# First softmax stage of a graph network: edge attributes read in turned order, logits left in PSUM, row numbers kept on chip

## The chip, the cores and the metric

The kernel runs on one core of one Trainium2 chip. The metric is the device time of one execution in microseconds. "Before" is the kernel as it stood; its median over three runs is 21826.02 us (21825.98 to 21843.0). All times are of these runs, or of one profiled execution of the same kernel.

## What is computed

Four graph layers run one after the other over the same graph of 12500 nodes and 212500 edges, each followed by a residual sum and a layer norm. The change touches the second layer only:

```python
h   = node_h @ W_fc.T                      # 12500 x 64
eh  = edge_h @ W_fcr.T                     # 212500 x 64, edge_h = edge_attr_64
alpha = _segment_softmax(eh, dst, N)       # per node and per feature
agg = segment_sum(alpha * (h[src] + eh), dst, N)
h_new = where(deg > 0, agg + h @ loop_W, h)
return relu(h_new)
```

The edges come sorted by `dst`. All arithmetic is float32.

## The kernel before

The program is a sequence of phases with a barrier between them. Edges are padded to 128 x 1664: partition p holds 1664 consecutive edges (`NT = 1664`), and an edge phase walks over its columns in chunks. The phase of interest is `softmax_made("L1", ...)`, which takes `TL = 26` columns of every partition at a time, so 128 x 26 edges a chunk and `NC = 64` chunks. It forms the edges' logits by a matmul and makes a running softmax along each partition, so that each node's maximum and sums stand at its last edge. Each engine has its own loop over the chunks; two chunks (buffers 0 and 1) stand in one loop body. Semaphores set the order.

- **SP** (SyncE) issues all ordinary transfers of a chunk: `side` (the edge attributes, [128, 26, 64], L1724), `idx` (the 26 row numbers of the source nodes, L1732), the store of `M` (running maxima, L1736) and of `DN` (running sums, L1738). The order in the queue is: side and idx of chunk n, then M and DN of chunk n-2, then side and idx of chunk n+1, and so on. The idx load waits until the gathers of chunk n-2 have landed; the store of DN waits for ACT's copies.
- **POOL** (GpSimd) issues 26 indirect gathers a chunk in `gathers` (L926), one for each column: 128 rows of 256 bytes of the table `tab`, into `rows[b]`. It waits first for the idx transfer and until `rows[b]` was used (`valued`, chunk n-2). The same helper and the same line serve the other edge phases.
- **PE** (TensorE) transposes 13 blocks of 128 x 128 a chunk (two edge columns each; `turn`, L1764, into `pt`), in four groups of 4, 4, 4 and 1 blocks, and multiplies each turned block by a block-diagonal weight `bd["fcr"]` (`multiply`, L1773, into `lg`). A float32 multiply of one block is two pairs of instructions, weight load and matmul; a transpose is one pair. `pt` and `lg` have two buffers of one group each.
- **ACT** (ScalarE) copies each turned group from PSUM to `attrT` (`take`, L1793) and each product from PSUM to `eh[b]` (`make`, L1800), for the chunk ahead. Between them it does its part for the current chunk: `fades` (Relu and Exp, L1810 to L1815), `kill` (L1805), and `back` (two copies of the sums into `DN`, L1822).
- **DVE** (VectorE) runs a chain for each chunk: copy `eh` into `lx` in turned order (L1874), scan for the running maximum (L1878), `M` (L1882), `rows + logits` into `PV` (L1886, needs the gathered rows), difference (L1889, counts `dk`), then, after ACT's Exp, the weighting (L1894) and two scans (L1899), and the carried column (L1902, L1871).

The four groups of a chunk are interleaved on PE and ACT like this:

```python
def step(i, b):                               # PE
    pe.wait_ge(side_in[b], (i + 1) * 16)
    turn(i, b, 0)
    for g in range(NGR):
        if g + 1 < NGR:
            turn(i, b, g + 1)
        multiply(i, b, g)
```

A kernel of the same build is the last softmax phase, `softmax_flat("L3", ...)` (L1509 on): same chunk of 26 columns, same gathers (512-byte rows), same stores, but its logits are a difference of two loaded arrays and PE has no part in it.

If the edges did not come sorted, `sort_by_dst` would sort them and permute all edge arrays first. Whether it runs is decided on the device (L2379).

Of the kernel before, what the change touches and what calls it, by code (L numbers as in the profile page):

```python
# [5 lines left out]
I32 = mybir.dt.int32  # L6
# [13 lines left out]
T = 64  # L20
NT = -(-E // (P * 2 * T)) * 2 * T
# [11 lines left out]
def gnn_resnorm(nc, x_in, src_0, dst_0, attr3_0, attr64_0, w_0, w2_0, W, out):  # L33
# [36 lines left out]
    attr3_in, attr64_s = dram("attr3_d", [EP, 3]), dram("attr64_d", [EP, F])  # L70
    w_in, w2_in = dram("w_d", [EP]), dram("w2_d", [EP])
# [1035 lines left out]

    def sort_by_dst():
# [13 lines left out]
        permute("attr64", attr64_0, attr64_s)  # L1122

# [556 lines left out]
    TL = 26  # L1680

    @phase
    def softmax_made(name, idx_arr, table, last, lastmax):
# [5 lines left out]
        idx_in, rows_in, side_in = S("idx"), S("rows"), S("side")  # L1689
# [4 lines left out]
        turned, at_hand, product, made = q("turned"), q("at_hand"), q("product"), q("edge_logits")  # L1694
        GR = [(4 * g, min(4, TL // 2 - 4 * g)) for g in range(-(-TL // 8))]
        NGR = len(GR)
        with ExitStack() as c, nc.Block() as block:
            idx = [alloc(c, f"idx{b}", [P, TL], I32) for b in range(2)]
            rows = [alloc(c, f"rows{b}", [P, TL, F]) for b in range(2)]
            side = [alloc(c, f"side{b}", [P, TL, F]) for b in range(2)]  # L1700
            eh = [alloc(c, f"eh{b}", [P, TL, F]) for b in range(2)]
            aT_ = [alloc(c, f"attrT{z}", [P, 4, P]) for z in range(2)]
            pt, lg = ([ps(c, f"{n}{z}", [P, 4, P]) for z in range(2)] for n in ("pt", "lg"))
# [13 lines left out]
            def _(sp):  # L1717
                def load(i, b):
                    ch = i * 2 + b

                    def attr(array):
                        if not isinstance(i, int) or i:
                            sp.wait_ge(turned, (ch - 1) * NGR)
                        sp.dma_start(side[b][:, :, :], cols(array, ch, TL)).then_inc(side_in[b], 16)  # L1724
                    with sp.If(in_order > P - 1):
                        attr(attr64_0)
                    with sp.Else():
                        attr(attr64_s)
                    sp.end_ifs()
                    if not isinstance(i, int) or i:  # L1730
                        sp.wait_ge(rows_in[b], i * 16 * TL)
                    sp.dma_start(idx[b][:, :], cols(idx_arr, ch, TL)).then_inc(idx_in[b], 16)  # L1732

                def store(ch):
# [3 lines left out]
                    sp.dma_start(cols(sums2[0:EP, :], ch, TL), DN[:, :, :]).then_inc(sstored, 16)  # L1738
                load(0, 0)
# [11 lines left out]
            @block.gpsimd  # L1751
            def _(pool):
                gathers(pool, table, idx, rows, idx_in, rows_in,
                        lambda e, i, b: e.wait_ge(valued, i * 2 + b - 1), go, TL, NC)

            @block.tensor
            def _(pe):
                def turn(i, b, g):
                    h0, n = GR[g]
                    if not (isinstance(i, int) and i == 0 and b == 0 and g < 2):  # L1760
                        pe.wait_ge(at_hand, (i * 2 + b) * NGR + g - 1)
                    for h in range(n):
                        r = side[b][:, 2 * (h0 + h):2 * (h0 + h) + 2, :].rearrange("p a f -> p (a f)")
                        t = pe.transpose(pt[g % 2][:, h, :], r, ident[:, :])  # L1764
                    t.then_inc(turned, 1)

                def multiply(i, b, g):
                    n = (i * 2 + b) * NGR + g
                    pe.wait_ge(at_hand, n + 1)
                    if not (isinstance(i, int) and i == 0 and b == 0 and g < 2):  # L1770
                        pe.wait_ge(made, n - 1)
                    for h in range(GR[g][1]):
                        t = pe.matmul(lg[g % 2][:, h, :], aT_[g % 2][:, h, :], bd["fcr"][:, :], start=True, stop=True)  # L1773
                    t.then_inc(product, 1)
# [11 lines left out]
            def _(act):  # L1786
                def take(ch, g):
                    n = ch * NGR + g
                    w = GR[g][1]
                    act.wait_ge(turned, n + 1)  # L1790
                    if not (isinstance(ch, int) and n < 2):
                        act.wait_ge(product, n - 1)
                    act.activation(aT_[g % 2][:, 0:w, :], pt[g % 2][:, 0:w, :], ACT.Copy).then_inc(at_hand, 1)  # L1793

                def make(ch, b, g):
                    h0, w = GR[g]
                    act.wait_ge(product, ch * NGR + g + 1)
                    if g == 0 and not (isinstance(ch, int) and ch < 2):
                        act.wait_ge(formed, ch - 1)
# [738 lines left out]
```

## Time and profile before

| | |
|---|---|
| median of three runs | 21826.02 us |
| the profiled execution: its time | 21834.51 us |
| the profiled execution: its span | 21832.8 us |
| mean granted TensorE clock | 0.555 of full speed |
| POOL busy | 12097.6 us (55%) |
| DVE busy | 10276.4 us (47%) |
| PE busy / weight loads | 4275.1 us (20%) / 3247.4 us (15%) |
| ACT busy | 4673.7 us (21%) |
| traffic | 1517.57 MB, 70 GB/s in the mean |
| phase `softmax_made` | 12971.4 to 15917.8 us: 2946.4 us |

No engine is busy for most of the span. The busy share of an engine is a mean over some thirty phases which have different limits, so it says little about one of them; the phase of the change has to be read by itself. "Before" in a row means idle time of that engine just ahead of the instruction, and the arrow names what ended it. Releasers are inferred, and where a semaphore number was used for something else in an earlier phase, the name can be of that phase. Ends of matmuls are modelled.

### The profile page before, as it was taken

The page shows a single profiled execution, that of the slowest core. Times are in us where ns is not written, and L with a number is a line of the kernel's source. Part 1 is how long each engine was busy: PE and PEld are TensorE (multiplying, and loading weights), DVE is VectorE, ACT ScalarE, POOL GpSimd, SP SyncE. Part 2 cuts the span into 40 slices and gives each one's busy share as a digit, 9 for nine tenths or more (in the row PEclk, how much of TensorE's full clock was granted, in tenths as well). Part 3 has the DMA queues.
Part 4 walks back from the last instruction along what each step waited for, and adds up shares of the span by engine and source line. Part 5 has one row for each costly group of instructions (what it writes and reads, how often), then busy time and mean ns, then how long its engine had stood idle before and what let it go on. Part 6 is the DMA issues. An engine that isn't in the chain of part 4 may idle for free. (4 is left out here: it accounts for less than half of the span.)

```text
span 21832.8 us, 104239 instructions
## 1 busy us (share of the span) xinstructions
PE 4275.1 (20%) x22758; PEld 3247.4 (15%) x22758; DVE 10276.4 (47%) x18332; ACT 4673.7 (21%) x4961; POOL 12097.6 (55%) x12292
## 2 busy tenths in 40 slices
PE   1222224444434211111111111111111111100000
PEld 1111113333333210000000011111110000000000
DVE  4444445444444443333222235555555555567776
ACT  0100111111111002222233324333311111124442
POOL 4444443344343337776766655555555555467776
PEclk7555556766667655555555555555555555555555
DMA  2111111111111331111111113222222222234443
GB/s 63 37 37 36 35 41 50 46 39 47 39 48 43 121 141 53 53 52 52 48 53 54 52 56 94 94 94 94 91 62 65 64 64 64 57 108 141 141 141 111
DMA packets 583064, 1517.57 MB, mean 70 GB/s; under 512 B 276152, under 2 KB 276685, under 8 KB 539138
## 3 DMA queue, kind: packets, MB, share of 16 engines
q1 hardware_dynamic: 188414, 1028.89, 12.7%
q0 software_dynamic: 392160, 467.91, 9.9%
q10 hardware_dynamic: 2068, 16.12, 0.2%
q8 instruction: 146, 2.39, 0.0%
q14 instruction: 276, 2.26, 0.0%
HBM read 714.46 MB, written 803.57 MB: 70 GB/s over the span
## 5 line engine op out<-in xcount | busy, mean ns | idle before, releaser
L926 POOL DMA_INDIRECT rows<-tab,idx x6656 | 6650.0, 999 | 3734.1 <-issue 2170.6
L572 POOL DMA_INDIRECT moved_rows<-recs,sidx x1664 | 1619.0, 973 | 2361.9 <-DVE sidx L687 1863.5
L926 POOL DMA_INDIRECT rows<-in_x,idx x1664 | 1590.7, 956 | 1691.5 <-DMA idx<-src_d 1192.1
L926 POOL DMA_INDIRECT rows<-sums,idx x1664 | 1615.8, 971 | 722.5 <-issue 692.5
L1049 DVE TENSOR_REDUCE small<-SQ 128x16 f32<-128x1024 f32 x104 | 127.5, 1226 | 2929.9 <-ACT SQ L1032 1998.2
L989 PE MATMUL dist_ps<-dist_w,a3T 65*128 65x512 f32 x416 | 392.8, 1100 | 4463.9 <-issue 2694.3
L656 DVE CUSTOM_DVE_ANT_0 junk<-pV,ohh 128x98 f32<-128x98 f32 x1664 | 424.3, 255 | 1387.4 <-remote 1142.5
L2344 DVE TENSOR_TENSOR_SCAN own<-held,lastu,own 128x64 f32<-128x64 f32 (+1 forms) x1690 | 517.7, 341 | 951.5 <-issue 942.0
L321 DVE TENSOR_TENSOR oh_dl<-dig_dl,held 128x2048 bf16<-128x2048 uint16 (+1 forms) x104 | 237.6, 2285 | 1486.4 <-remote 994.2
L1773 PE MATMUL lg<-bd_fcr,attrT 128*128 128x128 f32 x1664 | 408.5, 421 | 2331.5 <-ACT attrT L1793 1477.4
L609 ACT ACTIVATE place<-pP 128x98 f32<-128x98 f32 x832 | 210.7, 253 | 2961.7 <-remote 1375.1
L1027 ACT ACTIVATE yT<-dist_ps 128x512 f32<-128x512 f32 x208 | 124.1, 597 | 3201.3 <-PE dist_ps L1000 2438.5
L989 PEld LDWEIGHTS dist_ps<-dist_w,a3T 65*128 65x128 f32 x416 | 122.1, 324 | 4608.9 <-issue 4511.5
L648 DVE TENSOR_TENSOR same<-pE,mask 128x384 bf16<-128x384 f32 x832 | 442.3, 553 | 754.9 <-remote 570.1
L758 PE MATMUL pV<-place,ohT 128*128 128x98 f32 x1664 | 388.9, 319 | 1919.3 <-issue 1019.8
L1029 ACT ACTIVATE Y<-dist_ps 128x512 f32<-128x512 f32 x208 | 124.2, 597 | 2911.0 <-DMA after<-sums,elast 1484.3
L1351 DVE TENSOR_TENSOR_SCAN FB<-mask,FB 128x1430 f32<-128x1430 f32 x156 | 463.7, 3027 | 534.1 <-ACT FB L1324 334.8
L1773 PEld LDWEIGHTS lg<-bd_fcr,attrT 128*128 128x128 f32 x1664 | 360.0, 317 | 2383.9 <-ACT attrT L1793 1508.5
L746 PE MATMUL pE<-ohT 128*128 128x256 f32 x1664 | 628.5, 465 | 260.8 <-issue 225.4
L336 PE MATMUL H_d<-oh_dl,oh_dh 128*98 128x128 bf16 x1664 | 386.7, 305 | 1483.6 <-issue 968.4
L1005 PE MATMUL dist_ps<-dist_b,ones_row 1*128 1x512 f32 x416 | 393.4, 1043 | 1361.6 <-issue 1283.0
L1874 DVE COPY lx<-eh 128x1664 f32<-128x1664 f32 x64 | 119.4, 1866 | 1015.1 <-ACT eh L1800 954.0
(462 smaller groups left out, 19874.2 us busy)
## 6 DMA issues: line engine op xcount, KB each, us to landing
sums<-DN SPq DMA_DIRECT2D x128, 1664.0 KB
rows<-tab,idx POOLq DMA_INDIRECT x6656
spread<-zeros SPq DMA_DIRECT2D x52, 1040.0 KB
own<-spread SPq DMA_DIRECT2D x26, 2080.0 KB
sums<-rows SPq DMA_DIRECT2D x26, 2048.0 KB
dists<-Y SPq DMA_DIRECT2D x104, 512.0 KB, 2.7
recs<-sums SPq DMA_DIRECT2D x26, 2048.0 KB, 16.5
sums<-OUT SPq DMA_DIRECT2D x26, 2048.0 KB
```

The source lines that it names most:

```text
L336: last = pe.matmul(self.H[o][0:HI, :], oh[o + "h"][:, t, :], oh[o + "l"][:, t, :], start=False, stop=False, skip_group_check=True)
L572: pool.indirect_dma_start(moved_rows if fill else rec, bass.IndirectOffsetOnAxis(ap=idx[b][:, j:j + 1], axis=0), recs[b][:, j, :], None).t ...
L648: dve.tensor_tensor(same[g % 2][h][:, :, :], pE[h][:, :, :], mask[:, :, :], ALU.mult).then_inc(msk, 1)
L656: dve.tensor_tensor_reduce(out=junk[:, :], in0=pV[h][:, k, 0:HI], in1=ohh[b][:, t, :], scale=1.0, scalar=0.0, op0=ALU.mult, op1=ALU.add, a ...
L746: pe.matmul(pE[h][:, 0:2, :].rearrange("p a e -> p (a e)"), o[:, 2 * h, :], o[:, 2 * h:2 * h + 2, :].rearrange("p a e -> p (a e)"), start= ...
L758: pe.matmul(pV[h][:, 0, 0:HI], o[:, 2 * h, :], place[:, :], start=True, stop=False)
L926: pool.indirect_dma_start(rows[b][:, j, :], None, table, bass.IndirectOffsetOnAxis(ap=idx[b][:, j:j + 1], axis=0)).then_inc(rows_in[b], 16)
L989: t = pe.matmul(self.p1[:, 8 * h:8 * h + 8, :].rearrange("p a f -> p (a f)"), self.a3T[:, :], dist_w[:, h * 512:(h + 1) * 512], start=True ...
L1005: pe.matmul(self.p2[:, :, :].rearrange("p a f -> p (a f)"), ones_row[:, :], dist_b2[:, :], start=True, stop=False)
L1351: t = dve.tensor_tensor_scan(x, mask_flat[:, 0:(f1 - f0) * TB], x, 0.0, ALU.mult, ALU.add)
L1773: t = pe.matmul(lg[g % 2][:, h, :], aT_[g % 2][:, h, :], bd["fcr"][:, :], start=True, stop=True)
L2344: t = dve.tensor_tensor_scan(u[:, :, f], k, u[:, :, f], lastu[:, f:f + 1], ALU.mult, ALU.add)
```

## The change

The host hands over `edge_attr_64` a second time, turned: as [128, EP/2], where row `64 * a + f` and column `(h, p)` hold feature f of edge `2h + a` of partition p. A chunk of it is [128, 13 x 128], with 6656 consecutive bytes in each of 128 rows, as many as `side` had. In `softmax_made`

- SP loads this chunk into `attr_T[b]`; the load waits for PE's product of chunk n-2. The idx load of each chunk is gone; one load of all row numbers, `every` [128, 1664], stands ahead of the loop.
- PE makes no transposes. It waits for the transfer and until DVE has taken the logits of the chunk before (`formed`), and then multiplies 13 blocks in one go into a single `lg` of four PSUM banks.
- ACT makes no `take` and no `make` copies. It copies 26 row numbers from `every` to `idx[b]` (`pick`) in `fades`, behind the wait for `dk`, for the chunk two ahead.
- DVE copies the logits from `lg` straight to `lx`.
- POOL waits for `valued` as before and for `picked` in place of the idx transfer.

The unsorted path gets a new phase `turn_attr`, which makes the turned array on the device.

```diff
+    @phase
+    def turn_attr(table, to):
...
+                    for h in range(TL // 2):
+                        t = pe.transpose(pt[b][:, h, :], side[b][:, 2 * h:2 * h + 2, :].rearrange("p a f -> p (a f)"), ident[:, :])
...
         permute("attr64", attr64_0, attr64_s)
+        turn_attr(attr64_s, attr64T_s)
...
+            every = alloc(c, "every", [P, NT], I32)
             rows = [alloc(c, f"rows{b}", [P, TL, F]) for b in range(2)]
-            side = [alloc(c, f"side{b}", [P, TL, F]) for b in range(2)]
-            eh = [alloc(c, f"eh{b}", [P, TL, F]) for b in range(2)]
-            aT_ = [alloc(c, f"attrT{z}", [P, 4, P]) for z in range(2)]
-            pt, lg = ([ps(c, f"{n}{z}", [P, 4, P]) for z in range(2)] for n in ("pt", "lg"))
+            attr_T = [alloc(c, f"attrT{b}", [P, TL // 2, P]) for b in range(2)]
+            lg = ps(c, "lg", [P, 16, P])
+            eh = lg[:, 0:TL // 2, :].rearrange("p h (a f) -> p (h a) f", f=F)
...
-                            sp.wait_ge(turned, (ch - 1) * NGR)
-                        sp.dma_start(side[b][:, :, :], cols(array, ch, TL)).then_inc(side_in[b], 16)
+                            sp.wait_ge(product, ch - 1)
+                        sp.dma_start(attr_T[b].rearrange("p h e -> p (h e)"), array[:, bass.ds(ch * W2, W2)]).then_inc(side_in[b], 16)
...
-                    if not isinstance(i, int) or i:
-                        sp.wait_ge(rows_in[b], i * 16 * TL)
-                    sp.dma_start(idx[b][:, :], cols(idx_arr, ch, TL)).then_inc(idx_in[b], 16)
...
+                sp.dma_start(every[:, :], idx_arr.rearrange("(p t) -> p t", p=P)).then_inc(every_in, 16)
...
+                def gather(i, b):
+                    if not isinstance(i, int) or i:
+                        pool.wait_ge(valued, i * 2 + b - 1)
+                    pool.wait_ge(picked, i * 2 + b + 1)
+                    pool.sem_inc(go, 1)
+                    for j in range(TL):
+                        pool.indirect_dma_start(rows[b][:, j, :], None, table,
+                                                bass.IndirectOffsetOnAxis(ap=idx[b][:, j:j + 1], axis=0)).then_inc(rows_in[b], 16)
...
                 def step(i, b):
                     pe.wait_ge(side_in[b], (i + 1) * 16)
-                    turn(i, b, 0)
-                    for g in range(NGR):
-                        if g + 1 < NGR:
-                            turn(i, b, g + 1)
-                        multiply(i, b, g)
+                    if not isinstance(i, int) or i or b:
+                        pe.wait_ge(formed, i * 2 + b)
+                    for h in range(TL // 2):
+                        t = pe.matmul(lg[:, h, :], attr_T[b][:, h, :], bd["fcr"][:, :], start=True, stop=True)
+                    t.then_inc(product, 1)
...
+                def pick(ch, b):
+                    act.activation(idx[b][:, :], every[:, bass.ds(ch * TL, TL)], ACT.Copy).then_inc(picked, 1)
+
-                def fades(ch):
+                def fades(ch, b):
                     p = PV[:, 0, :, 1:TB]
                     act.wait_ge(dk, ch + 1)
+                    if not isinstance(ch, int) or ch < NC - 2:
+                        act.wait_ge(rows_in[b], (ch - b + 2) * (8 * TL))
+                        pick(ch + 2, b)
                     act.activation(p, lx[:, :, 1:TB], ACT.Relu, scale=-1.0).then_inc(act_step, 1)
...
-                    take(ch + 1, 0)
-                    take(ch + 1, 1)
-                    make(ch + 1, 1 - b, 0)
-                    fades(ch)
-                    take(ch + 1, 2)
-                    make(ch + 1, 1 - b, 1)
-                    take(ch + 1, 3)
-                    make(ch + 1, 1 - b, 2)
-                    make(ch + 1, 1 - b, 3)
+                    fades(ch, b)
                     kill(ch + 1)
                     back(ch)
...
-                    dve.wait_ge(made, (ch + 1) * NGR)
-                    dve.tensor_copy(l, eh[b][:, :, :]).then_inc(formed, 1)
+                    dve.wait_ge(product, ch + 1)
+                    dve.tensor_copy(l, eh).then_inc(formed, 1)
```

## Rows read from the trace of the kernel before

**Rows 1.** Busy time by engine (count of instructions) over the whole phase `softmax_made`.
```profile
core 0: us, PE busy (x) PEld busy (x) DVE busy (x) ACT busy (x) POOL busy (x), PEclk, DMA share, GB/s
12971.40:15917.80 2946.40, 565.13 (x2496) 510.62 (x2496) 1575.72 (x775) 1148.05 (x961) 1619.08 (x1664) 0.54 0.30 93
```
**Rows 2.** Waits of the phase, longest first: total us, times, longest us.
```profile
ACT eh L1800 <- DMA dists<-Y: 1055.9, 92, 21.4
DVE lx L1874 <- ACT eh L1800: 954.0, 30, 32.9
...
POOL rows L926 <- DMA idx<-src_d: 787.8, 32, 28.2
POOL rows L926 <- issue: 510.5, 1632, 2.4
```
**Rows 3.** Timeline, one pair of chunks: start us, us, engine, instruction, idle before.
```profile
14430.20 0.94 POOL L926 DMA_INDIRECT rows<-tab,idx  x1 [0.30 <-issue]
14435.54 0.60 ACT L1800 ACTIVATE eh<-lg 128x512 f32<-128x512 f32 x1 [18.63 <-DMA dists<-Y]
...
14456.60 0.94 POOL L926 DMA_INDIRECT rows<-tab,idx  x1 [25.46 <-DMA idx<-src_d]
...
14468.35 1.83 DVE L1874 COPY lx<-eh 128x1664 f32<-128x1664 f32 x1
...
14477.32 1.61 PE L1773 MATMUL lg<-bd_fcr,attrT 128*128 128x128 f32 x8
...
14489.56 7.67 DVE L1899 TENSOR_TENSOR_SCAN PV<-lx,PV 128x1792 f32<-128x1792 f32 x2 [1.15 <-ACT lx L1815]
```
**Rows 4.** The same timeline, ACT alone, from the middle of that pair on.
```profile
14476.71 0.60 ACT L1800 ACTIVATE eh<-lg 128x512 f32<-128x512 f32 x1 [1.68 <-PE lg L1773]
14482.94 1.61 ACT L1810 ACTIVATE PV<-lx 128x1728 f32<-128x1728 f32 x1 [5.63 <-DVE lx L1889]
...
14504.97 0.60 ACT L1800 ACTIVATE eh<-lg 128x512 f32<-128x512 f32 x1 [15.01 <-DMA dists<-Y]
14508.47 0.28 ACT L1793 ACTIVATE attrT<-pt 128x128 f32<-128x128 f32 x1 [2.90 <-DMA dists<-Y]
14527.39 0.60 ACT L1800 ACTIVATE eh<-lg 128x512 f32<-128x512 f32 x1 [18.64 <-DMA dists<-Y]
```
**Rows 5.** Timeline of an earlier phase (`sum_pass`): PE's matmuls beside POOL's gathers.
```profile
1282.82 0.27 PE L336 MATMUL H_s<-oh_sl,oh_sh 128*98 128x128 bf16 x1 [0.36 <-issue]
...
1285.78 0.31 PE L336 MATMUL H_d<-oh_dl,oh_dh 128*98 128x128 bf16 x1
1285.89 0.31 PE L336 MATMUL H_s<-oh_sl,oh_sh 128*98 128x128 bf16 x1
...
1324.86 0.95 POOL L926 DMA_INDIRECT rows<-in_x,idx  x1 [49.34 <-DMA idx<-src_d]
...
1395.55 0.27 PE L336 MATMUL H_s<-oh_sl,oh_sh 128*98 128x128 bf16 x1 [2.53 <-issue]
1398.35 0.27 PE L336 MATMUL H_d<-oh_dl,oh_dh 128*98 128x128 bf16 x1 [2.54 <-issue]
```
**Rows 6.** Groups of instructions in the phase: count, busy us, mean ns, idle before.
```profile
L1773 PE MATMUL lg<-bd_fcr,attrT 128*128 128x128 f32 x1664 | 408.5, 421 | 2331.5 <-ACT attrT L1793 1477.4 <-issue 854.1
...
L1882 DVE TENSOR_TENSOR M<-Hp,lx 128x1664 f32<-128x1664 f32 x64 | 205.0, 3203 | 7.7
```
**Rows 7.** Timeline: the phase's first and last instructions, and the next phase's first.
```profile
12977.36 0.94 POOL L926 DMA_INDIRECT rows<-tab,idx  x1 [28.24 <-DMA idx<-src_d]
...
15865.23 1.30 POOL L926 DMA_INDIRECT rows<-tab,idx  x1 [0.30 <-issue]
...
15885.43 3.15 DVE L1886 TENSOR_TENSOR PV<-rows,lx 128x1664 f32<-128x1664 f32 x1
...
15917.84 0.20 POOL L2008 MEMSET row<- 128x128 f32 x1 [51.31 <-SPq L1919]
```
**Rows 8.** The gathers of the last softmax phase (19340 to 21680), as a group.
```profile
L926 POOL DMA_INDIRECT rows<-tab,idx x1649 | 1747.0, 1059 | 538.5 <-issue 538.5
```

More of the change, by code:

```diff
@@ L20 @@
 T = 64
+TL = 26
 NT = -(-E // (P * 2 * T)) * 2 * T
@@ L1106, in _, with store, step @@
                 gathers(pool, table, idx, rows, idx_in, rows_in, lambda e, i, b: e.wait_ge(stored[b], i * 16), go, T, NCH)
+    @phase
+    def turn_attr(table, to):
+        W_ = TL // 2 * P
+        side_in, stored = ([sem(f"turn_{n}{b}") for b in range(2)] for n in ("in", "out"))
+        turned, copied = sem("turn_done"), sem("turn_copied")
+        with ExitStack() as c, nc.Block() as block:
+            side = [alloc(c, f"side{b}", [P, TL, F]) for b in range(2)]
+            out_ = [alloc(c, f"turned{b}", [P, W_]) for b in range(2)]
+            pt = [ps(c, f"pt{b}", [P, 16, P]) for b in range(2)]
+            @block.sync
+            def _(sp):
+                def store(ch, i, b):
+                    sp.wait_ge(copied, ch + 1)
+                    sp.dma_start(to[:, bass.ds(ch * W_, W_)], out_[b][:, :]).then_inc(stored[b], 16)
+                def step(i, b):
+                    ch = i * 2 + b
+                    if not isinstance(i, int) or i:
+                        sp.wait_ge(turned, ch - 1)
+                    sp.dma_start(side[b][:, :, :], cols(table, ch, TL)).then_inc(side_in[b], 16)
+                    if not isinstance(i, int) or i or b:
+                        store(ch - 1, i, 1 - b)
+                pairs(sp, step, NT // TL)
+                store(NT // TL - 1, 0, 1)
+                for b in range(2):
+                    sp.wait_ge(stored[b], NT // TL // 2 * 16)
+            @block.tensor
+            def _(pe):
+                def step(i, b):
+                    pe.wait_ge(side_in[b], (i + 1) * 16)
+                    if not isinstance(i, int) or i:
+                        pe.wait_ge(copied, i * 2 + b - 1)
+                    for h in range(TL // 2):
+                        t = pe.transpose(pt[b][:, h, :], side[b][:, 2 * h:2 * h + 2, :].rearrange("p a f -> p (a f)"), ident[:, :])
+                    t.then_inc(turned, 1)
+                pairs(pe, step, NT // TL)
+            @block.scalar
+            def _(act):
+                def step(i, b):
+                    act.wait_ge(turned, i * 2 + b + 1)
+                    if not isinstance(i, int) or i:
+                        act.wait_ge(stored[b], i * 16)
+                    act.activation(out_[b][:, :], pt[b][:, 0:TL // 2, :].rearrange("p h e -> p (h e)"), ACT.Copy).then_inc(copied, 1)
+                pairs(act, step, NT // TL)
     def sort_by_dst():
@@ L1688, in softmax_made @@
         q = lambda n: sem(f"{name}_{n}")
-        idx_in, rows_in, side_in = S("idx"), S("rows"), S("side")
+        every_in, picked, rows_in, side_in = q("every_in"), q("picked"), S("rows"), S("side")
         go, formed, edged, seen, maxed, dk, valued, weighed, summed, carried = (q(n) for n in (
@@ L1752, in _ @@
             def _(pool):
-                gathers(pool, table, idx, rows, idx_in, rows_in,
-                        lambda e, i, b: e.wait_ge(valued, i * 2 + b - 1), go, TL, NC)
+                def gather(i, b):
+                    if not isinstance(i, int) or i:
+                        pool.wait_ge(valued, i * 2 + b - 1)
[4 more added lines that the diff above has]
+                                                bass.IndirectOffsetOnAxis(ap=idx[b][:, j:j + 1], axis=0)).then_inc(rows_in[b], 16)
+                pairs(pool, gather, NC)
             @block.tensor
             def _(pe):
[L1758 to L1774, printed above, removed]
                 def step(i, b):
                     pe.wait_ge(side_in[b], (i + 1) * 16)
-                    turn(i, b, 0)
-                    for g in range(NGR):
-                        if g + 1 < NGR:
-                            turn(i, b, g + 1)
-                        multiply(i, b, g)
+                    if not isinstance(i, int) or i or b:
+                        pe.wait_ge(formed, i * 2 + b)
+                    for h in range(TL // 2):
+                        t = pe.matmul(lg[:, h, :], attr_T[b][:, h, :], bd["fcr"][:, :], start=True, stop=True)
+                    t.then_inc(product, 1)
                 pairs(pe, step, NC)
@@ L1786, in _ @@
             def _(act):
[L1787 to L1799, printed above, removed]
-                    act.activation(eh[b][:, 2 * h0:2 * (h0 + w), :].rearrange("p a f -> p (a f)"),
-                                   lg[g % 2][:, 0:w, :].rearrange("p a f -> p (a f)"), ACT.Copy).then_inc(made, 1)
                 def kill(ch):
```

28 lines of the change are left out of this document (11 added, 17 removed).

## The prediction

> **What bounds the kernel now.** The first view is the busy time by engine over the phase that is changed [rows 1]: in 2946.4 us no engine is busy for more than 55% of it, so waits set its length. The second is the list of waits [rows 2]. POOL's 1664 gathers take 1619.1 us, and 510.5 us pass between them, together 2129.6 us or 33.3 us a chunk. POOL also waits 787.8 us in 32 times for row numbers; 28.2 us of that is the wait at the start, most of it in the phase before. That leaves 31 holds, one for every second chunk, of 24.5 us, in sum 760 us. The phase is then 6.0 us to the first gather, 2129.6 of gathers, 760 of holds and 51.3 from the last gather's end to the next phase [rows 7]: 2946.9, which closes the account. Everything else lies beside POOL. What the change is worth is what it does to the holds and to the last piece.
>
> Why does POOL hold? The third view, the timeline of a pair of chunks [rows 3, 4], shows DVE's chain of one chunk undisturbed: from the copy of the logits at 14468.35 to the end of the last scans at 14497.2, and with 0.7 us of carried columns 29.8 us. That is less than 33.3. But every second chunk DVE waits some 32 us for ACT's copies of the products, and these wait for "DMA dists", a name left from an earlier phase; the only semaphore in these instructions is PE's. PE's matmuls are recorded in a bunch at 14477.3, and ACT's copy of that product starts at 14504.97; the next group's copy comes at 14527.39, 18.6 us after the copy of the last turned block. So PE is late, though its records, whose ends are modelled, look early. 18.6 us for four blocks, 16 weight loads and matmuls, is 1.16 us for one instruction, 0.86 a microsecond.
>
> An earlier phase shows the same on PE's own rows [rows 5]: while POOL gathers, one weight load and matmul take 2.80 us (0.71 instructions a microsecond), evenly, with nothing waited for; in POOL's hold they take 0.11 us. The slow pace outlasts the gathers: POOL stopped at 1324.86 - 49.34 = 1275.5, at 1282.8 PE was still slow, at 1285.8 fast. In the changed phase POOL's last gather ended at 14431.1 and the late copy came at 14435.5. And PE lives for a while on a stock: POOL resumed at 14456.60, and the copy at 14476.71 was on time, after 52 of PE's loads and matmuls (groups 3 and 4 of one chunk, two groups of transposes, one of products); 20.1 us at 0.86 brings 17 of them, so at least 35 had been ready. My reading: PE is fed with instructions slowly while POOL issues gathers, and catches up in the holds. Before, PE needs 39 pairs, 78 such instructions, a chunk; 33.3 us bring 29.
>
> The Trainium skill, "Runtime: NRT & Kernel Launch", section "Instruction fetch mechanics", says the opposite of this: the sequencer fetches the next block by itself while it works on the current one, and that is mostly hidden. By that rule PE would never be late and rival A below would be the time. The trace speaks against it, since nothing but supply is left to explain an even 2.80 us for a pair that takes 0.11 elsewhere.
>
> **The change, part by part.** *Transposes and ACT's copies go.* Per chunk PE loses 13 pairs and keeps 26, as the 1664 matmuls of L1773 over 64 chunks show [rows 6]: 52 instructions, with 4 waits and loop steps 56. ACT loses 8 copies, 0.28 to 0.60 us each, none of which bounds once PE is no longer served by them. That the groups are no longer handed to and fro removes no issue of PE's but its waits.
>
> *PE can't run ahead.* `lg` is single, and the product of a chunk starts only when DVE has taken the last one (1.9 us into DVE's chain). 56 instructions at 0.86 take 65 us while POOL gathers; natively 52 take 26 x 0.20 = 5.2 us (eight pairs in 1.61) [rows 3]. Product of chunk n+1 then lies beside the rest of DVE's chain of n. Behind PE's wait stands nothing but that product; DVE waits for it.
>
> *Row numbers.* POOL no longer depends on SP's queue. `every` has 832 KB like one `side` load and goes ahead of it; row numbers were there 6.0 us into the phase [rows 7], and I leave 6.0 for all of it and the first pick. In the loop, `pick` stands on ACT behind `dk`: it costs one small copy ahead of Relu, 0.28 us like the 128x128 copy [rows 4], between 0.1 and 0.6 (the 512 columns), on DVE's chain: 30.1 us, still under 33.3. POOL's gather of chunk n+2 now waits for chunk n's `dk`. With rows landed in time that is far ahead of POOL's need, so it costs nothing, unless PE is late: then POOL is held until 14.9 us after the product (14468.35 to 14482.94 and the pick) [rows 3, 4]. The 13 KB transfer and SP's wait for the gathers go, and with them nothing of the other transfers, which keep their sizes and order; SP moves on earlier.
>
> *Logits from PSUM.* The copy to `lx` takes 1.83 us from SBUF. From PSUM I take the same; at worst it costs what a strided read of PSUM and one of SBUF cost together, 3.2 us [rows 6]. The chain would be 31.5 us, still hidden by POOL. Not below 1.8, since the elements are the same.
>
> *The unsorted path* is not run: its permutations would show as further gathers.
>
> **The sum.** PE needs 56 instructions a chunk and gets 0.86 x 33.3 = 28.6 while POOL gathers; 27.4 are missing. They run out of the stock, PE falls back, and POOL is held. A hold lasts until PE has finished under slow supply (0 to 10 us by rows 3 and 5; I take 8) and 14.9 us more: 23 us. In it PE gets the next product whole, 56, and its stock back. The stock is at least 35; I take 45. One hold so pays for (56 + 45) / 27.4 = 3.7 chunks, 17 holds in the phase, 391 us in place of 760. The last gather's rows now are waited for at once: 32.4 us from L1886 to the next phase [rows 7], and 3 for landing, 35.4 in place of 51.3 (between 32.4 and 51.3). New phase: 6.0 + 2129.6 + 391 + 35.4 = 2562 us, 384 less. The profiled execution of 21834.5 us would be 21450; the median lies 8.5 us under it: 21441, say 21440.
>
> With 1 instruction a microsecond, a stock of 60 and 20 us, 116 / 22.7 = 5.1 chunks a hold, 12 holds, 243 us: 21290. With 0.71, 35 and 24.9 us, 91 / 32.3 = 2.8, 22 holds, 560 us: 21610.
>
> **Rivals.** *A, POOL is never held.* PE's slowness comes from the handing to and fro or from ACT's and SP's share, and goes with them. Then 6.0 + 2129.6 + 35.4 = 2171 us: 21050. If the gathers slow down beside denser stores to the 1.386 us of the last softmax phase, which is never held [rows 8], they take 2306 us: 21227. For it: that phase runs like this with the same DVE work. Against: PE has no part there, and rows 5 has no handing.
>
> *B, a hold still every second chunk.* The stock is lost at each loop's turn or a hold pays for two chunks only: 31 holds of 23 us, 713 us: 21763. For it: that is today's pattern. Against: 56 instructions instead of 78.
>
> *C, slower.* PE's supply is slow by itself and not by POOL, and PE has lost its room to run ahead. Each chunk is then 1.9 + 52 x 1.16 = 62.2 us, the phase 62.2 x 64 + 41 = 4022 us: 22900. It decides from the point where a product takes over 44 us, 46.0 us being today's chunk. Against: in holds PE is fast [rows 5].
>
> **How the numbers follow.** Forecast 0.57 (21290 to 21610), A 0.21, B 0.11, C 0.07, other gains 0.04. The range of 21040 to 21640 takes in the forecast and nearly all of A; it leaves out B, C and the end of A. A measurement tells 0.2%, 44 us, from no change: faster 0.88, same 0.05 (the slow end of B), slower 0.07.
>
> **What would show it.** In the phase's waits: POOL held some 17 times, for 20 to 25 us, in place of 31, and behind ACT's pick; none in A, 31 in B. DVE's copy of the logits waiting for PE ahead of each hold. PE's product taking under 8 us in or just behind a hold and over 30 us elsewhere. L1773's successor with 1664 matmuls, no L1764, no copies to `attrT` and `eh`. The gathers still at 1.25 to 1.4 us from start to start. The forecast is wrong if POOL runs through, if the copy from PSUM is far over 3.2 us, or if holds stay with PE's products early, which would put the row numbers' new path at fault.

## The result and the profile after

Kernel before: 21834.51 us (four runs, 21825.98 to 21849.27). Changed kernel: 21529.08 us (four runs, 21485.76 to 21557.08). The ratio is 0.9858, interval 0.9837 to 0.9878: 1.4% faster. The profiled execution took 21505.72 us, its span 21504.0. The forecast for the median was 21440 us; 21529 lies inside its range of 21040 to 21640. But this holds for the chip that both kernels ran on. The experiments come to a second chip with a kernel before as slow, where only variants of the change ran, and to four others, where the kernel before takes 16500 us; on the one of them that ran the changed kernel, the change is worth nothing.

The stage (the phase `softmax_made`) after, as windows by engine (the columns of [rows 1]), and its waits (the view of [rows 2]):

```profile
12957.20:15590.97 2633.77, 337.73 (x1664) 324.39 (x1664) 1572.48 (x775) 923.66 (x513) 1609.04 (x1665) 0.55 0.30 104
```
```profile
PE lg L1817 <- DVE lx L1887: 1609.8, 44, 63.5
ACT idx L1828 <- DVE lx L1902: 1064.4, 46, 48.5
...
DVE lx L1887 <- DMA dists<-Y: 582.0, 31, 39.5
POOL rows L1806 <- issue: 504.0, 1633, 2.5
POOL rows L1806 <- ACT idx L1828: 489.3, 31, 32.9
```

The stage is 2633.8 us in place of 2946.4, 312.6 less of the 328.8 by which the span is shorter. POOL still waits 31 times for row numbers, now behind ACT's pick. 32.9 us of it is the wait at the start, so 30 holds remain with 456.4 us in sum, 15.2 each (one pause of 2.5 us more stands in the view under "issue"); before there were 31 of 24.5. PE has lost the 832 turned blocks, and ACT 448 of its 961 instructions.

One long and one short hold in the timeline (POOL, DVE, PE and ACT picked out; in brackets the idle time before):

```profile
13806.00 1.90 DVE L1887 COPY lx<-lg 128x1664 f32<-128x1664 f32 x1 [7.65 <-DMA dists<-Y]
13807.95 4.64 PE L1817 MATMUL lg<-bd_fcr,attrT 128*128 128x128 f32 x26 [32.94 <-issue]
...
13853.83 0.94 POOL L1806 DMA_INDIRECT rows<-tab,idx  x1 [0.30 <-issue]
13864.11 1.90 DVE L1887 COPY lx<-lg 128x1664 f32<-128x1664 f32 x1 [28.23 <-DMA dists<-Y]
...
13878.82 0.23 ACT L1828 ACTIVATE idx<-every 128x26 int32 x1 [37.23 <-DVE lx L1902]
13879.83 0.94 POOL L1806 DMA_INDIRECT rows<-tab,idx  x1 [25.05 <-ACT idx L1828]
...
13893.98 1.84 DVE L1887 COPY lx<-lg 128x1664 f32<-128x1664 f32 x1
...
13936.33 1.90 DVE L1887 COPY lx<-lg 128x1664 f32<-128x1664 f32 x1 [12.50 <-DMA dists<-Y]
...
13952.06 0.94 POOL L1806 DMA_INDIRECT rows<-tab,idx  x1 [6.75 <-ACT idx L1828]
```

PE may start on a product when DVE's copy of the last one has ended, and its 26 matmuls are recorded right there, in 4.64 us. DVE gets the product only at 13864.11, 56.2 us after the copy that ended at 13807.90; its wait carries the stray name "DMA dists", as in [rows 2]. Read PE by this distance from copy to copy, not by its records. POOL had stopped at 13854.8; it goes on 15.7 us behind the product: DVE's chain up to L1902, the pick, the handing. In the hold the next product is there in time (13893.98, no wait); the one after takes 40.5 us (13895.82 to 13936.33) and costs a short hold of 6.75. So it goes through the stage: 16 holds of 12 us and more, and 14 of 4.6 to 9.7.

The trace has PE's semaphore for this product at 13864.09. It can't tell a late multiply from a late signal behind it, and no run does. The input of a late product was not late: for the one that DVE got at 13806.00, the load was issued at 13738.79 and had landed 4.1 us later, while PE could begin at 13770.29 at the earliest.

The costs of the parts, as groups over the stage (mean ns of one before the second bar):

```profile
L1817 PE MATMUL lg<-bd_fcr,attrT 128*128 128x128 f32 x1664 | 337.7, 393 | 2237.0 <-DVE lx L1887 1609.8 <-issue 615.5 <-DMA attrT<-in_attr64T 11.7
L1887 DVE COPY lx<-lg 128x1664 f32<-128x1664 f32 x64 | 120.1, 1876 | 679.6 <-DMA dists<-Y 582.0 <-issue 90.6 <-PE lg L1817 7.0
L1828 ACT ACTIVATE idx<-every 128x26 int32 (+1 forms) x64 | 14.3, 225 | 1266.9 <-DVE lx L1902 1064.4 <-issue 193.8 <-DMA every<-src_d 8.6
```

And its end:

```profile
15532.23 0.94 POOL L1806 DMA_INDIRECT rows<-tab,idx  x1 [0.31 <-issue]
15532.40 2.03 DVE L1902 TENSOR_TENSOR lx<-lx,Hp 128x1792 f32<-128x1792 f32 x1
...
15558.58 3.15 DVE L1899 TENSOR_TENSOR PV<-rows,lx 128x1664 f32<-128x1664 f32 x1
```

At the last gather DVE is still in the chunk before the last, and takes the last rows 26.3 us later. From the last gather's end at 15533.2 to the next stage pass 57.8 us.

### The profile page after: what moved, and what is told of

It reads as the page before. It is cut to its first block and busy times, and to the rows that moved or that the text cites. A ratio compares the mean times of both kernels' runs of the same rounds, so it can differ in the third digit from the quotient of the medians.

```text
span 21504.0 us, 100941 instructions
## 1 busy us (share of the span) xinstructions
PE 4035.1 (19%) x21926; PEld 3050.5 (14%) x21926; DVE 10270.1 (48%) x18332; ACT 4448.0 (21%) x4513; POOL 12074.0 (56%) x12292
## 5 line engine op out<-in xcount | busy, mean ns | idle before, releaser
L1817 PE MATMUL lg<-bd_fcr,attrT 128*128 128x128 f32 x1664 | 337.7, 393 | 2237.0 <-DVE lx L1887 1609.8
```

The source lines that it names most:

```text
L1817: t = pe.matmul(lg[:, h, :], attr_T[b][:, h, :], bd["fcr"][:, :], start=True, stop=True)
```

## Experiments on the slowing chip

The first four kernels ran on one chip, where the kernel before takes 21894.78 us. Their rows show the same holds and the same slow PE, so this chip is counted with the first; whether it is the same one is not on record. They vary what PE is given (e1 to e3) and what POOL issues (e4). Each was run once, with a profile; the changed kernel itself was not run on this chip, so each stage is compared with the changed kernel's stage from the first chip.

**Four blocks in one matmul.**

```diff
-                    for h in range(TL // 2):
-                        t = pe.matmul(lg[:, h, :], attr_T[b][:, h, :], bd["fcr"][:, :], start=True, stop=True)
+                    for h in range(0, TL // 2, 4):
+                        k = min(4, TL // 2 - h)
+                        t = pe.matmul(lg[:, h:h + k, :].rearrange("p h e -> p (h e)"), bd["fcr"][:, :],
+                                      attr_T[b][:, h:h + k, :].rearrange("p h e -> p (h e)"), start=True, stop=True)
```

> The changed kernel, but TensorE holds the block-diagonal weights and streams four 128-column blocks of turned edge attributes through them at once: 7 products of 128x512 or 128x256 in a chunk instead of 26 of 128x128, so about 16 TensorE instructions a chunk instead of 56. The columns multiplied are the same. The logits land in PSUM in another layout, so this first softmax stage computes with misplaced logits and its output is not the reference's; everything else is done as before, with the same number and size of operations. Theory S (while GpSimd issues indirect gathers, TensorE is supplied with about 0.86 instructions per us, 28.6 in the 33.3 us of a chunk's gathers, and GpSimd is held because TensorE falls behind): 16 is under 28.6, TensorE never falls behind, the 30 holds of 456 us in all vanish, the stage takes about 2634 - 456 = 2178 us and the profiled execution about 21505.7 - 456 = 21050 us. Rival L (each chunk's products arrive a fixed time late, or the hold is the ring of handings product, form, scan, M, valued, row numbers, whatever TensorE does): the holds stay at 15 us each, 21500 us. Between 21150 and 21400 neither is whole.

Measured: 21254.04 us. (The trace has 8 loads and 8 matmuls a chunk, not 7 products.) POOL's groups and those of DVE's copy, over the stage:

```profile
L1806 POOL DMA_INDIRECT rows<-tab,idx x1664 | 1753.5, 1054 | 585.8 <-issue 557.3 <-ACT idx L1830 28.5
L1818 PE MATMUL lg<-attrT,bd_fcr 128*128 128x512 f32 (+1 forms) x512 | 332.2, 816 | 1949.0 <-issue 1547.0 <-DVE lx L1889 390.3 <-DMA attrT<-in_attr64T 11.7
L1889 DVE COPY lx<-lg 128x1664 f32<-128x1664 f32 x64 | 117.7, 1839 | 6.9 <-PE lg L1818 6.9
```

The 28.5 us are the wait at the start: no hold is left, and DVE waits 6.9 us for products in the whole stage, with PE as busy as before the edit (332 us against 338). So the holds are made by the number of PE's instructions, not by its multiplying. Whether the weight loads or the matmuls count is not told apart: both fall together, and weights and attributes have changed places in the call. The time lies between the two expected cases (21050 and 21500), where the expectation called neither whole. The stage loses 282 us (2351.4 are left), not 456: the gathers now take 1753.5 + 557.3 = 2310.8 us, 1.389 from start to start in place of 1.270. That is the pace of the last softmax phase [rows 8], which is never held either. Why they slow down is not shown; never being held is not enough, as the other chips below show.

**Two blocks in one matmul.** The same edit with 2 for 4.

> As the run with four blocks, but two blocks at once: 13 products in a chunk, about 28 to 30 TensorE instructions, still misplaced logits in this stage. Theory S puts this at the balance point (28.6 supplied in 33.3 us): few and short holds, between 0 and 150 us in all, 21050 to 21200 us. If the supply counts instructions, it lies between the kernel with 56 and the one with 16, and near the latter. Rival L: 21500 us. Rival Bytes (it is not the count of instructions but the multiplying work, or TensorE's reads of SBUF against the gathers' writes, that is slowed): columns streamed are unchanged and so is the time.

Measured: 21296.15 us, a stage of 2397.2. POOL and DVE over the stage, and two copies of the timeline:

```profile
L1806 POOL DMA_INDIRECT rows<-tab,idx x1664 | 1637.8, 984 | 721.7 <-issue 503.8 <-ACT idx L1830 216.7 <-DVE PV L1901 1.2
L1889 DVE COPY lx<-lg 128x1664 f32<-128x1664 f32 x64 | 120.8, 1887 | 428.9 <-DMA dists<-Y 409.4 <-issue 12.6 <-PE lg L1818 7.0
```
```profile
13761.46 1.90 DVE L1889 COPY lx<-lg 128x1664 f32<-128x1664 f32 x1 [9.34 <-DMA dists<-Y]
...
13777.25 0.94 POOL L1806 DMA_INDIRECT rows<-tab,idx  x1 [6.37 <-ACT idx L1830]
13800.77 1.90 DVE L1889 COPY lx<-lg 128x1664 f32<-128x1664 f32 x1 [9.43 <-DMA dists<-Y]
```

With 28 loads and matmuls a chunk there are 33 holds of 5.7 us. A product takes 37.4 us (13763.36 to 13800.77), and nearly the same in many chunks: 0.75 instructions a microsecond, 2.67 us for a pair. From copy to copy pass 39.3 us, and 14 pairs at the 2.80 us of [rows 5] are 39.2: PE gets a pair every 2.80 us, 0.71 instructions a microsecond, through POOL's pauses of 6.3 us too. With 16 instructions a product takes 4.5 to 6.0 us in the 31 chunks whose semaphore the trace has, and in the others DVE did not wait for it. The time is near that of the kernel with 16, as expected, but 96 us over the expected range of 21050 to 21200.

**More waits, no more work.**

```diff
     t = pe.matmul(lg[:, h, :], attr_T[b][:, h, :], bd["fcr"][:, :], start=True, stop=True)
+    for _ in range(4):
+        pe.wait_ge(side_in[b], 16)
```

> The changed kernel, and TensorE issues four more waits after each of the 26 products of a chunk, on a count that the semaphore already has: 104 more instructions a chunk, no more multiplying. Output unchanged. Theory S, each wait counted as an instruction: TensorE needs 160 a chunk and is supplied with 28.6 beside the gathers; GpSimd is held at nearly every one of 62 chunks, each for the supply's lag of up to 10 us, the rest of the instructions at the quick pace of 5 to 10 per us (6 to 20 us) and the 9 us handing: 25 to 40 us a hold, 1550 to 2500 us in all, total 22600 to 23500 us. Rival L, or multiplying work as the cause: satisfied waits cost some 0.05 us each at most, hidden beside the gathers: 21500 us.

The expectation counted wrongly: a chunk has 13 calls, so 52 waits were added; part of them became instructions of their own, two behind each call, 26 a chunk. Measured: 21379.35 us, a stage of 2467.6.

```profile
L1806 POOL DMA_INDIRECT rows<-tab,idx x1664 | 1620.1, 974 | 806.7 <-issue 497.7 <-ACT idx L1830 309.0
```

PE has half as many instructions again, and the holds do not grow; they shrink, from 456 us to 281 (309.0 less the start). They are now regular, one of 7 to 12 us at every second chunk after a first one of 25. The time misses both expected cases (22600 to 23500, and 21500). Theory S in the form "every instruction is supplied slowly" falls: waits on PE's sequencer add nothing, weight loads and matmuls are slow. That waits between them help is not shown by one run beside a changed kernel from the first chip; if they do, the reason is open.

**Plain DMAs in place of indirect gathers.**

```diff
-pool.indirect_dma_start(rows[b][:, j, :], None, table,
-                        bass.IndirectOffsetOnAxis(ap=idx[b][:, j:j + 1], axis=0)).then_inc(rows_in[b], 16)
+pool.dma_start(rows[b][:, j, :], table[0:P, :]).then_inc(rows_in[b], 16)
```

> The changed kernel, but in this one stage GpSimd issues 26 plain DMAs a chunk, each reading the first 128 rows of the table into the place where the indirect gather of 128 rows would land: same bytes, same semaphores, no index read; this stage's rows are therefore the wrong ones and the output is not the reference's. It asks whether the slow supply of TensorE belongs to GpSimd's indirect gathers or to any DMAs in flight. Theory S-gather: plain DMAs are issued without the table look-up, GpSimd takes well under 1 us for each, TensorE's 26 products come in 5 to 10 us throughout, and the stage is bound by the DVE chain of 30 us a chunk, 64 x 30 = 1920 us: total about 20800 us. Theory S-any (any descriptor building by GpSimd, or the traffic itself, starves TensorE): products stay slow, 0.7 to 1 instruction per us, the stage takes over 2600 us.

Measured: 20837.87 us. Window, POOL and DVE's copy over the stage:

```profile
12981.70:14912.00 1930.30, 336.99 (x1664) 323.82 (x1665) 1566.10 (x775) 927.54 (x513) 875.54 (x1665) 0.56 0.41 142
```
```profile
L1806 POOL DMA_DIRECT2D rows<-tab x1664 | 875.5, 541 | 1010.7 <-ACT idx L1827 987.1 <-issue 23.6
L1886 DVE COPY lx<-lg 128x1664 f32<-128x1664 f32 x64 | 117.7, 1839 | 7.2 <-PE lg L1816 7.2
```

The DMA engines move more per microsecond than in any other kernel (142 GB/s; 104 in the changed one), with the same 1664 matmuls as in the changed kernel, and DVE never waits for one past the start. A product takes 4.6 to 6.0 us. So it is POOL's *indirect* gathers that slow PE, not the rate of the traffic. The edit changes two more things: POOL reads the same 128 rows each time, and issues for 0.54 us in place of 0.97. The stage is DVE's chain, 1930.3 us; 1920 had been expected.

PE is not the only one. SP's issue of the load of the turned attributes is recorded at 0.35 us each time with plain DMAs, but at over 0.65 us in 51 of 64 cases with four blocks, in 57 with two and in 27 in the changed kernel. First with four blocks, then with plain DMAs:

```profile
13832.47 0.70 SPq L1773 DMA_DIRECT2D attrT<-in_attr64T  x1
```
```profile
13835.52 0.35 SPq L1773 DMA_DIRECT2D attrT<-in_attr64T  x1
```

The waits and branches of ACT and DVE are as short as on the other chips.

## Experiments on chips that do not slow PE

The next eight kernels ran on four other chips. Their kernel before takes 16502 to 16522 us. First the changed kernel itself:

> The changed kernel as it is, once more, beside the kernel before on the same chip. The four runs of the last group came from a chip on which the kernel before takes 16503 us in place of 21826, GpSimd's 1664 gathers in this stage follow each other without a hold, and every variant is within 0.2% of before. Theory P (the whole gain of the change is that TensorE, slowed while GpSimd issues gathers, has less to do; where it isn't slowed, the change has nothing to give): on such a chip the ratio is 1.000, between 0.998 and 1.002, and the stage takes 6 + 1664 gathers + 36 us, about 2130 us, in both kernels. On a chip of the first kind (before near 21850 us) it is 0.984 to 0.988, some 30 holds, 300 to 330 us gained in the stage. Rival: the copies that ACT and TensorE no longer do give something by themselves: under 0.997 also on a chip of the second kind.

Measured: 16512.29 us against 16513.47, ratio 1.0005, interval 0.9996 to 1.0015. The change does nothing that can be told apart here. The stage as window and its POOL waits:

```profile
9403.00:11538.30 2135.30, 340.79 (x1664) 327.57 (x1665) 1570.08 (x775) 926.53 (x513) 1586.15 (x1665) 0.56 0.41 128
```
```profile
POOL rows L1806 <- issue: 506.7, 1663, 0.3
...
POOL rows L1806 <- ACT idx L1828: 28.6, 1, 28.6
```

2135 us, 6.3 to the first gather, 2092.8 of gathers, 35.9 behind them, no hold. PE's product takes 4.6 to 6.0 us each time, and SP's issue of the load 0.35. The gathers run at 1.258 us from start to start, though POOL is never held. The earlier stage `sum_pass` of [rows 5] tells the chips apart most plainly; PE's waits in it, in the same program, first on the first chip, then on this one:

```profile
PE H_d L338 <- issue: 938.0, 359, 16.3
PE H_s L338 <- issue: 635.4, 331, 3.2
PE H_d L338 <- DVE oh_sh L323: 542.1, 78, 17.5
```
```profile
PE H_d L338 <- DVE oh_sh L323: 751.6, 104, 17.5
```

The 1573 us in which PE waited for nothing that the profile shows are gone. One gather costs nearly the same on both, 967 ns and 953, so POOL's own speed is no sign of it.

**Single parts and reorderings.** These divide the gain on a slowing chip into its parts, or try to enlarge it. All of them ran on chips that don't slow PE, where they can't answer that. Two were run on two chips each.

The row numbers' DMA put back (L1828 and `every` out, the 13 KB load on SP in):

> The changed kernel with its third part undone: the row numbers of a chunk come by a 13 KB DMA on SP's queue as before, instead of a copy on ACT behind dk; turned loads and logits from PSUM stay. Output unchanged. Theory H (in a hold the handing counts: the pick stands 2.6 us behind valued, the DMA is issued at the product and has landed by valued): each of 30 holds ends 2.6 us sooner, 78 us: 21430 us by the profiled run of after, ratio to before near 0.982. Rival Q (the row numbers' DMA lands late, behind the stores of sums and M on the same queue, as in the kernel before, where it was issued 14448.1 and GpSimd went on at 14456.6): holds 3 to 6 us longer each, 90 to 180 us, 21600 to 21690, ratio 0.990 to 0.994.

16509.87 us, ratio 1.0003, interval 0.9994 to 1.0013.

The row numbers' pick alone, in the kernel before:

> The kernel before with the third part alone: all row numbers loaded once and picked by ACT behind dk; transposes, copies and the handing between TensorE and ACT stay. Output unchanged. Theory H: a hold of before ended when the row numbers' DMA landed, 21 us after ACT's copy of the late product began; with the pick it ends 18 us after: 31 holds 3 us shorter, 93 us, about 21740 us, ratio near 0.9957. The whole change gave 320 us, so the other two parts would hold the rest. Rival: GpSimd's gathers or TensorE, not the handing, set the period of 92 us for two chunks, and what a hold loses comes back in the next one: 21826, ratio 1.000.

> The run e6_pick_only once more (the kernel before with the row numbers picked by ACT; output unchanged), for the same reason. On a chip that slows TensorE, theory H: 31 holds 3 us shorter, 93 us, ratio near 0.9957; rival: what a hold loses comes back in the next one, ratio 1.000. On the other kind: within 0.1% of before again, ratio 0.999 to 1.002.

16524.63 us, ratio 1.0007 (0.9997 to 1.0016), and 16538.69 us, ratio 1.0008 (0.9998 to 1.0018). Its profile matters all the same: this kernel keeps the turned blocks, 78 loads and matmuls a chunk, with ACT's copies between them, and is not held either:

```profile
L1758 POOL DMA_INDIRECT rows<-tab,idx x1664 | 1611.7, 969 | 535.8 <-issue 506.9 <-ACT idx L1814 28.9
```

So on such a chip the handing between PE and ACT, by which the kernel before looked late, is not late by itself.

`valued` ahead of M and the pick ahead of the wait for `dk`:

```diff
-                    act.wait_ge(dk, ch + 1)
                     if not isinstance(ch, int) or ch < NC - 2:
                         act.wait_ge(rows_in[b], (ch - b + 2) * (8 * TL))
                         pick(ch + 2, b)
+                    act.wait_ge(dk, ch + 1)
...
                     if not first:
-                        dve.wait_ge(mstored, ch * 16)
-                    dve.tensor_tensor(M[:, :, :], by_edge(H_before[:, :, 1:TL + 1]), l, ALU.max).then_inc(maxed, 1)
-                    if not first:
                         dve.wait_ge(copied, ch * 2)
                     dve.wait_ge(rows_in[b], (i + 1) * 16 * TL)
                     dve.tensor_tensor(by_edge(PV[:, 1, :, 1:TL + 1]), rows[b][:, :, :], l, ALU.add).then_inc(valued, 1)
+                    if not first:
+                        dve.wait_ge(mstored, ch * 16)
+                    dve.tensor_tensor(M[:, :, :], by_edge(H_before[:, :, 1:TL + 1]), l, ALU.max).then_inc(maxed, 1)
```

> The changed kernel with two reorderings, output unchanged: on DVE, valued goes ahead of M, and on ACT the pick goes ahead of the wait for dk. A hold then ends about 9.3 us after the product (copy 1.9, scan 3.95, valued 3.2, handing 0.3) instead of 14.9. Theory H, holds count by their handing alone: 30 x 5.6 = 168 us less, 21340 us, ratio 0.977. Theory C (TensorE catches up only in a hold and a little after; what the hold is shortened by, it lacks later): the next hold comes sooner or is longer, and less than half of the 168 us is gained, 21420 to 21500 us, ratio 0.981 to 0.985.

> The run e8_both_early once more (valued ahead of M, the pick ahead of the wait for dk; output unchanged), since its question can only be put on a chip that slows TensorE (kernel before near 21850 us), and the first time it ran on one that doesn't. On the first kind, theory H: 168 us less than the changed kernel, 21340 us, ratio 0.977; theory C: less than half of that, 21420 to 21500 us, ratio 0.981 to 0.985. On the second kind: 16535 us and ratio 1.002 again, because the gathers were slower beside the new order of DVE's work (1612.7 us for 1664 against 1590.5 and 1580.6).

> The same two reorderings, with the satisfied waits of the run e3_waits52 on TensorE (four behind each of the 13 matmul calls of a chunk: 52 waits; the expectation of that run said 26 calls and 104 waits, which is wrong). Output unchanged. There a hold of 9.2 us stood at every second chunk, 281 us in all and 21379 us. Theory H: holds shrink by 5.6 us each, 168 us less, 21210 us, ratio about 0.968. Theory C: there the second product of each pair of chunks came 7.5 us into the hold; with the hold cut to 3.6 us it would come later and be waited for in turn, so little is gained: 21320 to 21400 us, ratio 0.974 to 0.978. If the waits had nothing to do with the 126 us by which e3_waits52 was faster, then as the run without them.

16535.91 us, ratio 1.0019 (1.0009 to 1.0029); again 16549.49, ratio 1.0017 (1.0008 to 1.0027); with the waits 16533.56, ratio 1.0018 (1.0009 to 1.0028). All three are a little slower than before, with nothing to gain where no hold is. In the profiles the gathers took 1612 us (1586 in the changed kernel); but they took 1580.6 and 1611.7 in two profiles of the pick alone, so the order of DVE's work is not shown to be the cause, as one expectation had it.

Fewer columns, the same number of instructions (`bd["fcr"][:, 0:16]` in the loop):

> The changed kernel, but from the third chunk on each of the 13 matmuls of a chunk multiplies 16 of the 128 columns of the weights: as many weight loads and matmul instructions as before (52 a chunk), an eighth of the streamed columns. The other logits stay those of the second chunk, so this stage and the output are not the reference's. On a chip that slows TensorE beside GpSimd's gathers (kernel before near 21850 us): if the number of instructions for the array counts, the holds stay as with 128 columns, 30 of 15 us, 21500 us; if the multiplying counts, none stays, 21050 to 21250 us as with the four-block products. On a chip that doesn't slow it (before near 16510 us) there is no hold in any case: 16510 us, and the run only says that once more.

16528.11 us, beside 16502.08, one run each: no hold, nothing told apart. That the columns don't count rests on the four-block and two-block runs alone.

## Why the prediction was right, point by point

Times in us; holds are their number and their sum.

| 1664 gathers in the stage | loads and matmuls a chunk | stage | holds | gathers | behind the last |
|---|---|---|---|---|---|
| before, first chip | 78 | 2946.4 | 31, 760 | 2129.6 | 51.3 |
| predicted | 52 | 2562 | 17, 391 | 2129.6 | 35.4 |
| after, first chip | 52 | 2633.8 | 30, 456 | 2113.0 | 57.8 |
| with added waits | 52 (and 26 waits) | 2467.6 | 30, 281 | 2117.8 | 62.9 |
| two blocks | 28 | 2397.2 | 33, 188 | 2141.6 | 59.6 |
| four blocks | 16 | 2351.4 | 0 | 2310.8 | 34.0 |
| after, other chip | 52 | 2135.1 | 0 | 2092.8 | 35.9 |
| pick alone, other chip | 78 | 2161.4 | 0 | 2118.6 | 36.6 |

**What bounds the stage: right.** POOL's holds, and behind them PE slowed beside POOL's gathers. Three runs on one chip, each taken once, show it: holds shrink with two blocks and go with four at the same multiplying, and DVE waits for no product where the DMAs are plain. The reading of [rows 5] was the decisive one. How much of the change's own gain comes from PE's 26 instructions less a chunk and how much from the pick is not shown; no run on a slowing chip divides them.

**Its mechanism, the supply of instructions: not shown, and partly wrong.** Waits pass freely beside slow matmuls. The rate of 0.86 a microsecond was too high; the two-block run has 0.71, as [rows 5] had. And there is no fetching in the loops: over 1300 us of the stage after (13300 to 14600) the DMA queues were these, with none of the kind "instruction", which the page of the whole execution does list:

```profile
q1 hardware_dynamic: 13574, 107.61, 21.5%
q0 software_dynamic: 26368, 27.05, 8.9%
```
```profile
q8 instruction: 157, 2.57, 0.1%
```

Both kinds of chip show 157 packets on that queue. The sentence of the Trainium skill set against the trace ("Runtime: NRT & Kernel Launch", "Instruction fetch mechanics") is therefore not contradicted: no fetch is seen in the loop at all. By it rival A would have been the time. On the first chip that was not the time; on the other chips POOL is never held, as A has it.

**The number and length of the holds: mis-sized, errors that partly cancel.** The stock failed. I took 45 instructions, from 52 that were on time behind a hold. But that stock is paid out once; beside gathers it does not fill so far. After a hold of 25 us the product after next took 40.5 us for its 52; at the 0.75 a microsecond of the two-block run these are 30, so some 22 had been ready (an estimate), and 16 were always in time. The two-block run gives some 30 at its start: seven products, 196 instructions, were there 229.6 us after the first gather (12983.0 to 13212.6), in which 0.71 brings 163. From then on its products take 37.4 us, so that little of the stock comes back. With 22 and 0.75, 25 come a chunk, 31 are missing, and a hold pays (56 + 22) / 31 = 2.5 chunks: 26 holds by the same formula, 30 measured. The formula is fitted behind the result here, and by it the two-block run would have had fewer holds than its 33. The length failed the other way: 23 us assumes that PE is entirely late. The long ones are so (9.3 until the product, 15.7 behind it, 25.0), but half are short, since a product that is 12 us late costs POOL 7. So 30 x 15.2 stands for 17 x 23, 65 us more. That the sum comes out so near, with 76% more holds of two thirds of the length, is luck.

**The end: wrong by 22 us.** I had the last gather's rows waited for at once. That holds where PE is not late (34.0 with four blocks, 35.9 on the other chip). With PE late DVE is a chunk behind when POOL ends, and a chain of 29.4 us comes on top (15529.15 to 15558.58 for the two uses of L1899).

**Small terms: right.** The copy from PSUM takes 1.88 us (1.84 where nothing disturbs; 1.83 forecast, up to 3.2 allowed), the pick 0.225 (0.28). From the start to the first gather pass 6.5 us (6.0). Gathers cost 16.6 us less. Sum: 65 + 22 + 0.5 - 16.6 = 71, the stage's 2634 against 2562.

**Rivals.** A, no hold, came in the four-block run, and with the gathers at 1.389 us as its second number had it: a stage of 6 + 2306 + 35.4 = 2347 us, 2351.4 measured. (Its 21227 beside the 21254 measured compares two chips.) C, PE slow by itself, is excluded: 4.6 to 6.0 us a product with plain DMAs, on a chip of the slow kind. B had the right number of holds, one for every second chunk on average, but not their length.

**What no step held:** that the slowness of PE belongs to the chip. The page before shows one chip, and its PE rows look like a property of the program.

Open: what in a chip slows loads and matmuls, and SP's issues with them; how the gain divides between fewer loads and matmuls and the pick; whether added waits help (0.9765 of before in one run, against 0.9858 for the change on the first chip), and if so why; and why pauses of 6.3 us in the two-block run bring PE nothing, when one of 6.75 us in the changed kernel was enough for its next product to be in time. None of the versions is faster than the kernel before on the other chips.

## What to carry to other kernels

An engine that is late with nothing to wait for, evenly and only beside another engine's work, may be so on this chip alone. Compare the kernel before and the changed one on a second chip before you tune to it: here the same edit is worth 1.4% or nothing. Where PE is slowed beside indirect gathers, count its loads and matmuls, and make them wider: the same columns in 16 instructions in place of 52 left no hold. And don't book a removed hold as a whole: 456 us of holds gone gave 282, since the gathers themselves took 198 us longer, and only 24 came back at the stage's end.

## What the runs showed of the hardware

- On two chips (or one, met twice) PE's loads and matmuls drop to 0.71 to 0.75 a microsecond while POOL issues indirect gathers, after a reserve that comes out at 20 to 30 (an estimate); with plain DMAs of the same bytes, 26 pairs come in 4.6 to 6.0 us. SP's issue of one load is then recorded at 0.70 us in place of 0.35. In eight profiles on four other chips no hold appears in the stage, and the same program takes 16.5 ms in place of 21.8.
- On the slowing chip 26 satisfied waits a chunk between matmuls cost nothing: 281 us of holds with them, 456 without on the first chip.
- Matmul records of a slowed PE are early: the last of a product ended at 13812.6 by its record, and DVE and the trace's semaphore have the product at 13864.1. When the next engine starts is the measure.
- An ACT copy of 128x26 integers takes 0.225 us, and DVE's strided copy of 128x1664 from PSUM 1.84 to 1.88.
